# Query and key projections made once per token in the row passes and spread by copies, with three second-pass matmuls issued ahead of a step's first-pass ones

## The chip, the cores and the metric

One core of one Trainium2 chip runs the whole program in one launch. The metric is device time in microseconds (us), from the first to the last instruction of the launch, as the median of several runs. The engines are called PE (TensorE, matrix products), DVE (VectorE), ACT (ScalarE), POOL (GpSimd) and SP (SyncE, which here only issues copies). They run side by side, each through its own list of instructions in order, and meet at semaphores.

## The reference

Four sequences of 1024 tokens, 128 channels, float32. Two attention layers of 16 heads of 8 channels, the first causal with a linear position bias, the second full, and then a mixture of eight experts:

```python
x = L0_attn_x                                    # (4, 1024, 128)
x = x + layernorm(attn_causal_alibi(layernorm(x)))
u = layernorm(x)
u1 = u + layernorm(attn_full(u)) * ln1_g + ln1_b
u2 = u1 + layernorm(moe_top2_of_8(u1)) * ln2_g + ln2_b
x = x + layernorm(u2)
# both attentions, for 16 heads of 8 channels:
q, k, v = u @ Wq + bq, u @ Wk + bk, u @ Wv + bv
p = softmax(q k^T / sqrt(8) (+ slope * (i - j), causal))
out = (p v) @ Wo + bo
```

## The kernel before, in words

The program has five parts. A **first row pass** (`rows_pass`, tag `first`) reads the input, normalizes it, turns it so that channels lie on partitions, makes the values and leaves the turned input for all 4096 tokens in `turned` (a high and a low part, since a product is made as three matmuls of float32r parts: `three`). **Attention 1** (`attention`, tag `at1`, causal) follows, then a **second row pass** (tag `second`: output projection, norms, residual, turning, values), **attention 2** (tag `at2`, full) and the **tail** (experts), which the change does not touch.

A row pass goes over 8 groups of 512 tokens. The order of steps on each engine comes from the tables `ONLY_SPLIT` (first pass) or `JOIN` and `SPLIT_OFF` (second pass): step `s` of group `n` is sorted at time `n + table[s]`, so an engine's list interleaves steps of several groups.

An attention works in 16 **slots**: a slot is one sequence with four heads (`GH = 4`). Its 32 rows per head in `fq` (queries) and `km` (keys) hold the 8 query or key channels three times (high and low parts), two rows of position bias and two for the maximum. Each slot needs

- four **projections** (`proj`: key and query for both halves of the 1024 tokens). On PE three matmuls of 512 columns into a bank of the ring `a_bank` (a key of attention 1 has a fourth, for the bias), on ACT one pass into `u` (L443), on POOL three passes that split it into high and low rows (L596, L599, L606), and for keys four copies of 64 KB by SP (L627) that put each head's rows into `km`;
- the **first pass**, matmuls `a` (L367, 64 per slot in attention 2, 40 in attention 1, where diagonal blocks add two mask matmuls each, L372): scores with queries on partitions, of which DVE takes the row maximum (L498). They use a ring of four banks, so an `a` waits until DVE has read the fourth before it;
- the **second pass**, matmuls `b` (L395): scores again, with keys on partitions and the maximum subtracted, exponentiated by ACT (L454). They have three banks, so a `b` waits for the exponential of the third before it;
- `pv` (L412): the weighted values, four heads side by side in eight PE instructions;
- `mtr` and `otr`, small transposes for the maximum and for the output, with a division on DVE (`at_rec`, L526).

`Plan.body` writes a slot's order out: 12 steps in attention 1, 16 in attention 2. A step has the four `b` of one block of 128 keys, two to five `a` (spread over the steps by `weights`), at four of the steps a projection for the slot three ahead, and the `pv` of two blocks back. The `a` of the early steps (0 to 6 in attention 1, 0 to 10 in attention 2) belong to the next slot, those of the later ones to the slot after it:

```python
            out += bs[:1] + ass + bs[1:]
            ...
            for n, at in enumerate(self.proj_steps):
                if at == i and do_proj:
                    out.append(("proj", 3, n))
```

`Plan.prologue` makes the projections of the first three slots and the first slot's `a`. The first three batches' slots run in a loop over batches; the last four (slots 12 to 15) are written out. Slots 13, 14 and 15 have no projection, since there is no slot three ahead, and slot 15 has no `a` either.

## Time and profile before

| | |
|---|---|
| median of 3 runs | 2212.74 us (2209.97 to 2213.57) |
| the profiled execution | 2207.67 us, of which 2206.0 us are the span of the trace |
| PE busy | 1947.8 us (88% of the span) |
| DVE busy | 1661.0 us (75%) |
| ACT busy | 1342.6 us (61%) |
| POOL busy | 844.8 us (38%) |
| copies | 39656 packets, 41.98 MB |

A bracket behind a row of the timeline gives the idle time just before it and which instruction ended it. "x4" means that four instructions in a row were merged.

### The profile page before, as it was taken

To read this page: it belongs to the slowest core of one execution; us is meant where nothing else is said; L and a number is where in the kernel's file an instruction comes from. 1 tells how busy PE (TensorE), PEld (TensorE's weight loads), DVE (VectorE), ACT (ScalarE), POOL (GpSimd) and SP (SyncE) were. 2 spreads that over 40 slices of the span, in tenths; PEclk is the share of its full clock that TensorE was granted. 3 is DMA by queue.
4 is the path that set the end of the run, shared out by engine and by line. 5 is a ranking of instruction groups with operands and counts; after the bars stand their busy time and mean duration, and the time that the engine had idled before them with its cause. 6 is when DMAs were issued, how large, how long until landed. Compare 5 with 4: busy or idle time off the path is not lost. (4 is left out here: it accounts for less than half of the span.)

```text
span 2206.0 us, 41897 instructions
## 1 busy us (share of the span) xinstructions
PE 1947.8 (88%) x11036; PEld 1037.6 (47%) x11036; DVE 1661.0 (75%) x3185; ACT 1342.6 (61%) x2647; POOL 844.8 (38%) x816
## 2 busy tenths in 40 slices
PE   5899899899997699999999899999964999999996
PEld 4444444454443443333333334333323666666664
DVE  5677677677753778887888788888804999898986
ACT  4266666566765427766677676777763655555563
POOL 4455455545311342222222222220003466665554
PEclk7699999999986659999999999999996999999998
DMA  2100000000001200000000000000002100000000
GB/s 64 28 17 16 17 16 16 17 14 18 11 1 48 77 19 11 11 11 12 11 15 12 12 11 11 11 10 6 1 15 68 34 20 20 20 16 4 19 10 10
DMA packets 39656, 41.98 MB, mean 19 GB/s; under 512 B 6361, under 2 KB 24934, under 8 KB 39426
## 3 DMA queue, kind: packets, MB, share of 16 engines
q1 hardware_dynamic: 38544, 38.90, 6.4%
q8 instruction: 103, 1.69, 0.3%
q14 instruction: 127, 1.04, 0.2%
q10 hardware_dynamic: 882, 0.36, 0.1%
HBM read 14.07 MB, written 6.29 MB: 9 GB/s over the span
## 5 line engine op out<-in xcount | busy, mean ns | idle before, releaser
L498 DVE TENSOR_REDUCE at_mx<-at_a 128x1 f32<-128x512 f32 (+3 forms) x1664 | 997.6, 662 | 269.1 <-PE at_a L367 199.3
L454 ACT ACTIVATE at_probs<-at_b 128x512 f32<-128x512 f32 (+3 forms) x1792 | 868.2, 557 | 450.1 <-PE at_b L395 444.8
L395 PE MATMUL at_b<-at_fqm,km 64*128 64x512 f32 (+3 forms) x1792 | 632.3, 445 | 52.0 <-ACT at_probs L454 33.5
L395 PEld LDWEIGHTS at_b<-at_fqm,km 64*128 64x128 f32 x1792 | 295.9, 190 | 513.3 <-ACT at_probs L454 406.5
L367 PE MATMUL at_a<-km,at_fq 64*128 64x512 f32 (+2 forms) x1664 | 489.6, 458 | 37.6 <-DVE at_mx L498 29.3
L412 PE MATMUL at_pv<-at_probs,at_vst 128*32 128x512 f32 (+3 forms) x3584 | 449.8, 576 | 1.7 <-POOL at_probs L579 1.7
L596 POOL TENSOR_TENSOR at_hi<-at_u,split_sign 128x512 fp32r<-128x512 f32 x120 | 124.6, 1038 | 460.4 <-ACT at_u L443 406.9
L367 PEld LDWEIGHTS at_a<-km,at_fq 64*128 64x128 f32 x1664 | 238.9, 195 | 126.2 <-DVE at_mx L498 95.8
L1228 ACT ACTIVATE t_hid<-t_bank_h,b1t 128x512 f32<-128x512 f32 x256 | 173.9, 688 | 196.9 <-DVE t_hid_lo L1362 113.0
L1362 DVE TENSOR_TENSOR t_hid_lo<-t_hid,t_hid_hi 128x512 fp32r<-128x512 f32 x256 | 227.3, 923 | 13.9 <-ACT t_hid_hi L1235 11.8
L1396 POOL TENSOR_TENSOR t_hid_hi<-t_hid,pow_cols 128x512 fp32r<-128x512 f32 x112 | 140.8, 1272 | 130.4 <-ACT t_hid L1228 129.8
L579 POOL TENSOR_SCALAR_AFFINE_SELECT at_probs<-at_probs 128x512 f32<-128x512 f32 x128 | 81.1, 634 | 238.1 <-ACT at_probs L454 238.1
L443 ACT ACTIVATE at_u<-at_a,bias 128x512 f32<-128x512 f32 x128 | 88.7, 693 | 104.3 <-PE at_a L218 63.8
L216 PE MATMUL t_bank_y<-t_hid_hi,t_w2hi 128*128 128x512 f32 x256 | 107.0, 418 | 30.5 <-DVE t_weighed L1371 26.3
L599 POOL TENSOR_TENSOR at_part<-at_hi,split_sign 128x512 f32<-128x512 f32 x120 | 124.8, 1040 | 21.8 <-POOL at_hi L596 21.8
L412 PEld LDWEIGHTS at_pv<-at_probs,at_vst 128*32 128x32 f32 x3584 | 72.1, 109 | 112.0 <-ACT at_probs L454 53.7
L218 PE MATMUL t_bank_y<-t_hid_hi,t_w2lo 128*128 128x512 f32 x256 | 103.0, 402 | 0.0
L217 PE MATMUL t_bank_y<-t_hid_lo,t_w2hi 128*128 128x512 f32 x256 | 102.3, 400 | 0.0
L372 PE MATMUL at_a<-half_mask,half_ident 64*128 64x128 bf16 (+1 forms) x768 | 93.1, 249 | 2.9 <-issue 2.9
L526 DVE RECIPROCAL at_rec<-at_a 128x16 f32<-128x16 f32 x64 | 16.3, 254 | 94.0 <-PE at_a L419 92.6
L561 POOL COPY at_vst<-tokens 128x256 f32 (+1 forms) x32 | 12.9, 402 | 193.4 <-PE at_pv L412 192.9
L606 POOL TENSOR_TENSOR at_fk<-at_part,at_u 128x512 fp32r<-128x512 f32 x60 | 76.4, 1274 | 19.7 <-POOL at_part L599 19.7
(210 smaller groups left out, 2377.5 us busy)
## 6 DMA issues: line engine op xcount, KB each, us to landing
km<-at_fk SPq DMA_DIRECT2D x256, 64.0 KB, 2.0
t_raw<-L_ffn_W SPq DMA_DIRECT2D x16, 256.0 KB, 3.1
x_first<-L_attn_x SPq DMA_DIRECT2D x4, 512.0 KB, 7.6
second_x_in<-L_attn_x SPq DMA_DIRECT2D x8, 256.0 KB, 3.4
kept<-second_joined SPq DMA_DIRECT2D x8, 256.0 KB, 2.5
kept_u<-second_normed SPq DMA_DIRECT2D x8, 256.0 KB, 2.0
t_heads_in<-tokens SPq DMA_DIRECT2D x8, 256.0 KB, 2.7
t_u_in<-kept_u SPq DMA_DIRECT2D x8, 256.0 KB, 2.9
```

The source lines that it names most:

```text
L216: pe.matmul(out, a[0], b[0], start=start, stop=False)
L218: return pe.matmul(out, a[1], b[0], start=False, stop=stop)
L367: mm = pe.matmul(scores, fq[g][rows, qt * P:(qt + 1) * P], km[g][rows, first:first + k, kh * HALF:kh * HALF + w], start=True, stop=not dia ...
L395: mm = pe.matmul(out[:, 0:w], km[g][rows, j % 2, kt * P:(kt + 1) * P], fqm[g % 2][rows, q0:q0 + w], start=True, stop=True)
L412: mm = pe.matmul(pv_bank[HW * j:HW * (j + 1), HALF - w:HALF], vst[g % 2][:, kt, j, :], probs[n % PROBS][:, j, 0:w], start=(kt == 0), stop= ...
L454: act.activation(probs[t % PROBS][:, j, 0:w], b_bank[n % B_BANKS][:, 0:w], ACT.Exp).then_inc(exp_done, 1)
L498: dve.tensor_reduce(mx[:, kh, qt, heads[0]:heads[0] + k], scores[:, 0:k * w].rearrange("p (k w) -> p k w", k=k), AX.X, ALU.max).then_inc(a ...
L596: pool.tensor_tensor(hi[:, :], un[:, :], split_sign[:, 2:3].broadcast_to([P, HALF]), ALU.add).then_inc(pool_step, 1)
L599: pool.tensor_tensor(part[:, :], hi[:, :].bitcast(F32), split_sign[:, m:m + 1].broadcast_to([P, HALF]), ALU.mult).then_inc(pool_step, 1)
L1228: act.activation(hid[:, f, :], h_bank[f][:, :], ACT.Gelu, bias=b1t[:, f, e:e + 1]).then_inc(hidden["act"], 1)
L1362: dve.tensor_tensor(hid_lo[e % 2][:, f, :], hid[:, f, :], hid_hi[e % 2][:, f, :].bitcast(F32), ALU.subtract).then_inc(hidden["dve"], 1)
L1396: pool.tensor_tensor(out, a, b, op).then_inc(stage["pool"], 1)
```

## The change

1. The row passes make the projections of all 128 channels once: per group three matmuls for `q` and three for `k` (128 columns of weights instead of 32 rows per head in four slots), one ACT pass each (`q_out`, `k_out`), the high and low parts of the queries on DVE (`q_hi`, `q_lo`) and of the keys on POOL (`k_hi`, `k_lo`). They are kept in four arrays `packed`. To make room among the eight banks, the head transposes, the values and each projection have one bank instead of two, and `turned` is now a pair of buffers.
2. In the attentions a slot's `fq` and `km` rows are filled by 24 copies of 8 rows by 1024 columns (32 KB each), issued by SP at the start of a slot for the slot three ahead (`load`). All 24 must have landed before the slot's first `a`. Projections leave PE, ACT, DVE, POOL and the ring of banks. The loads of the first three slots stand in the prologue.
3. The position bias rows of `km` are computed once at the end of the first row pass (three DVE passes) and put in place by 16 copies of 4 rows; constant rows of `fq` are filled by POOL.
4. A step issues three `b`, its `a`, and then the fourth `b`.

```diff
@@ class Plan @@
-        weights = [4 + .6 * (i in self.proj_steps) - (i in self.o_steps) - 1.5 * (i in self.mt_steps) - .5 * (i == self.m_step)
+        weights = [4 - (i in self.o_steps) - 1.5 * (i in self.mt_steps) - .5 * (i == self.m_step)
                    for i in range(nq)]
...
+        out = [("load", 3, 0)] if do_load else []
...
-            out += bs[:1] + ass + bs[1:]
+            out += bs[:3] + ass + bs[3:]
...
-        out = [("proj", 0, n) for n in range(4)]
...
-        out += self.interleave(ahead[:early], [("a", 0, c) for c in range(self.na)])
+        out = [("load", s, 0) for s in range(3)]
+        out += [("a", 0, c) for c in range(self.na)]
@@ attention, tensor @@
-                            done(pe, split_done, 4, s, 2 * (qt // HQ) + 1)
-                            done(pe, keys_spread[kh], KEYS, s, KEYS - 1)
+                        if n == 0:
+                            done(pe, loaded, LOADS, s, LOADS - 1)
@@ attention, sync @@
+                    if ds == 3:
                         done(sp, b_made, NB, s - 4, NB - 1)
-                    done(sp, split_done, 4, s, n)
+                    done(sp, loaded, LOADS, s - 1, LOADS - 1)
+                    tokens = bass.ds(b * T, T)
                     for j in range(GH):
...
+                        for c in range(3):
+                            rows = slice(HW * j + c * DH, HW * j + (c + 1) * DH)
+                            sp.dma_start(fq[g][rows, :].bitcast(F32),
+                                         packed["q", QUERY_PARTS[c]][head, tokens].bitcast(F32)).then_inc(loaded, 16)
+                            sp.dma_start(km[g][rows, j % 2, :].bitcast(F32),
+                                         packed["k", KEY_PARTS[c]][head, tokens].bitcast(F32)).then_inc(loaded, 16)
@@ the tables of the row passes @@
 ONLY_SPLIT = {
+    "pe": {"turn": 1.6, "values": 2.85, "q": 4.05, "k": 4.1},
+    "act": {"root2": .5, "norm2": .9, "turned": 2.6, "high": 3.55, "q_out": 4.3, "k_out": 4.35},
+    "dve": {"stats2": 0, "scale2": .6, "values": 3.55, "low": 3.8, "q_hi": 4.7, "q_lo": 4.75},
+    "pool": {"k_hi": 4.7, "k_lo": 4.8},
 }
 SPLIT_OFF = {
+    "pe": {"turn": 3.22, "values": 3.5, "q": 4.1, "k": 4.15},
+    "act": {"root2": 2.47, "norm2": 2.85, "turned": 3.35, "q_out": 4.3, "k_out": 4.35},
+    "dve": {"stats2": 2.15, "scale2": 2.52, "values": 3.8, "low": 3.95, "q_hi": 4.6, "q_lo": 4.65},
+    "pool": {"high": 3.55, "k_hi": 4.6, "k_lo": 4.7},
 }
@@ rows_pass, tensor @@
+                else:
+                    if n == 0:
+                        extra.get("weights", lambda _: None)(pe)
+                    after(pe, "dve", "low", n)
+                    after(pe, "act", f"{step}_out", n - 1)
+                    m = "qk".index(step)
+                    mm = three(pe, qk_bank[step][0][:, :, :].rearrange("p a b -> p (a b)"),
+                               [part[:, m, :] for part in wqk], [part[i][:, :] for part in turned])
@@ build, the first pass's extras @@
+                sp.wait_ge(fixed_step, 3)
+                for h in range(H):
...
+                    sp.dma_start(km[g][rows, j % 2, :].bitcast(F32),
+                                 fixed[4 * h:4 * h + 4, :].bitcast(F32)).then_inc(fixed_put, 16)
+                sp.wait_ge(fixed_put, 16 * H)
...
+                for q in fq:
+                    pool.tensor_tensor(q[:, :], query_col[:, 0:1].broadcast_to([P, T]),
+                                       pow_cols[:, 3:4].broadcast_to([P, T]), ALU.add)
```

How it moves instructions on **PE in attention 2**, in the written-out slot 12 (`at_a`, `at_b`, `at_pv` are the banks; of before, two steps, the second with a projection):

```order
L395 MATMUL at_b<-at_fqm,km 128x512
L367 MATMUL at_a<-km,at_fq 128x512 x4
L395 MATMUL at_b<-at_fqm,km 128x512 x3
L412 MATMUL at_pv<-at_probs,at_vst 32x512 x4
L395 MATMUL at_b<-at_fqm,km 128x512
L367 MATMUL at_a<-km,at_fq 128x512 x5
L395 MATMUL at_b<-at_fqm,km 128x512 x3
L216 MATMUL at_a<-turned_hi,w_hi 128x512
L217 MATMUL at_a<-turned_lo,w_hi 128x512
L218 MATMUL at_a<-turned_hi,w_lo 128x512
L412 MATMUL at_pv<-at_probs,at_vst 32x512 x4
```

The same two steps of the changed kernel:

```order
L362 MATMUL at_b<-at_fqm,km 128x512 x3
L334 MATMUL at_a<-km,fq 128x512 x5
L362 MATMUL at_b<-at_fqm,km 128x512
L379 MATMUL at_pv<-at_probs,at_vst 32x512 x4
L362 MATMUL at_b<-at_fqm,km 128x512 x3
L334 MATMUL at_a<-km,fq 128x512 x4
L362 MATMUL at_b<-at_fqm,km 128x512
L379 MATMUL at_pv<-at_probs,at_vst 32x512 x4
```

The three projection matmuls are gone, the `a` stand between the third and the fourth `b`, and the steps with five `a` are others: 0, 2, 4 and 6 of a slot instead of 1, 3, 4, 6 and 9.

On **PE in the second row pass** the projections come between a group's values and the next group's turn (`bank_h`: heads turned, `bank_y`: output projection, `bank_n`: normalized rows turned, `bank_v`: values, `bank_q` and `bank_k`: projections). One group of before:

```order
L754 MATMUL second_bank_n<-ident,second_normed 128x128 x4
L748 MATMUL second_bank_y<-wo,second_heads_t 128x128 x4
L759 MATMUL second_bank_v<-wv,second_turned_1 128x128 x4
L743 MATMUL second_bank_h<-ident,tokens 128x128 x4
```

and of the changed kernel:

```order
L673 MATMUL second_bank_n<-ident,second_normed 128x128 x4
L667 MATMUL second_bank_y<-wo,second_heads_t 128x128 x4
L678 MATMUL second_bank_v<-wv,second_turned_1 128x128 x4
L662 MATMUL second_bank_h<-ident,tokens 128x128 x4
L208 MATMUL second_bank_q<-second_turned_hi,wqk_hi 128x512
L209 MATMUL second_bank_q<-second_turned_lo,wqk_hi 128x512
L210 MATMUL second_bank_q<-second_turned_hi,wqk_lo 128x512
L208 MATMUL second_bank_k<-second_turned_hi,wqk_hi 128x512
L209 MATMUL second_bank_k<-second_turned_lo,wqk_hi 128x512
L210 MATMUL second_bank_k<-second_turned_hi,wqk_lo 128x512
```

The six new matmuls need the low part of their own group's turned rows, and the next turn now stands behind them.

On **DVE in the second row pass** one group's round in the changed kernel, from one group's low part to the next one's, reads:

```order
L776 TENSOR_TENSOR second_turned_lo<-second_turned_0,second_turned_hi 128x512
L761 BN_STATS second_stats<-second_joined 128x6 x4
L765 BN_AGGR second_mean_var<-second_stats 128x2 x4
L769 RECIPROCAL second_scale<-second_root 128x4
L771 SCALAR_TENSOR_TENSOR second_shift<-second_mean_var,second_scale 128x4
L769 RECIPROCAL second_scale<-second_root 128x4
L771 SCALAR_TENSOR_TENSOR second_shift<-second_mean_var,second_scale 128x4
L780 CAST packed_q_hi<-second_q_out 128x512
L784 TENSOR_TENSOR packed_q_lo<-second_q_out,packed_q_hi 128x512
L748 TENSOR_TENSOR second_y<-second_bank_y,bo 128x512
L788 TENSOR_TENSOR tokens<-second_bank_v,bv 128x512
L761 BN_STATS second_stats<-second_y 128x6 x4
L765 BN_AGGR second_mean_var<-second_stats 128x2 x4
L776 TENSOR_TENSOR second_turned_lo<-second_turned_1,second_turned_hi 128x512
```

New in it are the two rows that write `packed`; the rest has the order of before.

## Rows read from the trace of the kernel before

**Rows 1.** Busy time by stage: stretch, its length, busy us (instructions) per engine, clock, copies.
```profile
0.00:48.50 48.50, 24.29 (x128) 21.62 (x128) 28.83 (x102) 24.89 (x59) 22.44 (x41) 0.84 0.28 73
...
107.70:690.00 582.30, 541.09 (x4000) 273.73 (x3996) 397.58 (x739) 370.46 (x840) 260.98 (x301) 0.95 0.06 14
690.00:750.00 60.00, 35.03 (x192) 29.52 (x192) 43.37 (x186) 39.20 (x97) 18.51 (x16) 0.74 0.33 106
...
824.00:1645.00 821.00, 756.04 (x4400) 312.10 (x4400) 634.24 (x1097) 578.57 (x1096) 179.97 (x170) 0.99 0.04 10
```

**Rows 2.** Timeline, DVE: the division at the end of slots 11 to 13, both attentions.
```profile
555.38 0.26 DVE L526 RECIPROCAL at_rec<-at_a 128x16 f32<-128x16 f32 x1
...
590.74 0.25 DVE L526 RECIPROCAL at_rec<-at_a 128x16 f32<-128x16 f32 x1
...
622.06 0.25 DVE L526 RECIPROCAL at_rec<-at_a 128x16 f32<-128x16 f32 x1
...
1460.13 0.26 DVE L526 RECIPROCAL at_rec<-at_a 128x16 f32<-128x16 f32 x1
...
1511.33 0.26 DVE L526 RECIPROCAL at_rec<-at_a 128x16 f32<-128x16 f32 x1
...
1558.69 0.26 DVE L526 RECIPROCAL at_rec<-at_a 128x16 f32<-128x16 f32 x1
```

**Rows 3.** Timeline of a step without first-pass matmuls, slot 15 of attention 2.
```profile
1612.16 0.73 PE L395 MATMUL at_b<-at_fqm,km 64*128 64x512 f32 x3
...
1613.35 0.50 PE L395 MATMUL at_b<-at_fqm,km 64*128 64x512 f32 x1 [0.46 <-ACT at_probs L454]
...
1614.77 0.73 PE L395 MATMUL at_b<-at_fqm,km 64*128 64x512 f32 x3
```

**Rows 4.** Timeline of a step with five first-pass matmuls, slot 13 of attention 2.
```profile
1512.97 10.68 DVE L498 TENSOR_REDUCE at_mx<-at_a 128x1 f32<-128x512 f32 x17 [1.06 <-PE at_a L367]
...
1514.82 0.49 PE L395 MATMUL at_b<-at_fqm,km 64*128 64x512 f32 x1
...
1516.33 0.49 PE L367 MATMUL at_a<-km,at_fq 64*128 64x512 f32 x1 [0.33 <-DVE at_mx L498]
...
1517.99 0.50 PE L395 MATMUL at_b<-at_fqm,km 64*128 64x512 f32 x1
```

**Rows 5.** Issues on SP in the timeline, and landing time on the page.
```profile
1224.08 2.41 SPq L627 DMA_DIRECT2D km<-at_fk  x4
...
1647.18 0.33 SPq L1669 DMA_DIRECT2D select<-const_select  x1
...
km<-at_fk SPq DMA_DIRECT2D x256, 64.0 KB, 2.0
```

**Rows 6.** Timeline, PE, prologues: first first-pass matmuls, and one projection.
```profile
58.60 0.39 PE L367 MATMUL at_a<-km,at_fq 64*128 64x256 f32 x2 [1.83 <-DMA km<-at_fk]
...
63.16 0.80 PE L216 MATMUL at_a<-turned_hi,w_hi 128*128 128x512 f32 x1
...
65.27 0.80 PE L367 MATMUL at_a<-km,at_fq 64*128 64x512 f32 x2
...
759.25 0.78 PE L367 MATMUL at_a<-km,at_fq 64*128 64x512 f32 x4 [2.91 <-DVE at_fk L488]
```

**Rows 7.** Groups of the second row pass by form: busy us, mean ns.
```profile
L827 DVE BATCH_NORM_STATS2 second_stats<-second_y 128x6 f32<-128x128 f32 x32 | 6.9, 278 | 0.1
...
L842 DVE TENSOR_TENSOR turned_lo<-second_turned,turned_hi 128x512 fp32r<-128x512 f32 x8 | 6.3, 785 | 0.0
```

**Rows 8.** Timeline, DVE: the last row step of the first row pass.
```profile
44.16 0.68 DVE L842 TENSOR_TENSOR turned_lo<-first_turned,turned_hi 128x512 fp32r<-128x512 f32 x1
```

**Rows 9.** The page's issues: size, and median us from issue to landing.
```profile
x_first<-L_attn_x SPq DMA_DIRECT2D x4, 512.0 KB, 7.6
```

**Rows 10.** Timeline of the first row pass, DVE beside POOL.
```profile
21.98 3.73 POOL L1599 TENSOR_TENSOR w_hi<-w,pow_cols 128x1024 fp32r<-128x1024 f32 x2
...
22.57 3.17 DVE L837 SCALAR_TENSOR_TENSOR first_shift<-first_mean_var,first_scale 128x4 f32<-128x4 f32 x1
```

More of the change, by code:

```diff
@@ L94, in __init__ @@
         o0 = self.half_end[0] + 1
-        free = [i for i in range(1, nq - 4) if i != o0]
-        self.proj_steps = [free[len(free) * i // 4] for i in range(4)]
         self.o_steps = (o0, nq - 1)
@@ L436, in emit @@
                     s = s0 + ds
[L437 to L446 removed]
+                    if what == "b":
                         t, j = n // GH, B_HEADS[n % GH]
@@ L564, in emit @@
             def emit(steps, s0, b0, g0, places, before):
-                if steps[0][1] == 0 and steps[0][0] == "proj":
+                if places is in_prologue:
                     stage_values(0, 0)
@@ L773, in _ @@
                     after(act, "pe", "project", n - 2)
-                    op = act.activation(heads_t[i][:, :], h_bank[i][:, :, :].rearrange("p a b -> p (a b)"),
+                    op = act.activation(heads_t[i][:, :], h_bank[0][:, :, :].rearrange("p a b -> p (a b)"),
                                         ACT.Identity)
+                elif step in ("q_out", "k_out"):
+                    k, m = step[0], "qk".index(step[0])
+                    if n == 0:
+                        extra.get("weights", lambda _: None)(act)
+                    after(act, "pe", k, n)
+                    after(act, "dve" if m == 0 else "pool", f"{k}_lo", n - 2)
+                    op = act.activation(out[k][i][:, :], qk_bank[k][0][:, :, :].rearrange("p a b -> p (a b)"),
+                                        ACT.Identity, scale=1.0 if m else SCALE, bias=bqk[:, m:m + 1])
                 elif step.startswith("root"):
```

350 lines of the change are left out of this document (116 added, 234 removed).

## The prediction

> **What bounds the kernel now.** I read the busy time by stage first. The two attentions take 582 and 821 us, the row passes only 48.5 and 60 [rows 1]. In the attentions PE is busy 93% and 92% of the time at a clock near full, DVE 68% and 77%, ACT 64% and 70% [rows 1]. No engine's throughput alone sets the pace, so I looked at single steps. Then I looked for a piece of the program in which the change is already half made, and there is one: slots 13 to 15 have no projection. The division that ends a slot marks slot lengths on DVE. Slot 12, with four projections, takes 590.74 − 555.38 = 35.36 us in attention 1; slot 13, with the same `a`, `b` and `pv` and no projection, takes 31.32. In attention 2 it is 51.20 and 47.36 [rows 2].
>
> What sets a step without projections? In slot 15 of attention 2 there are no `a` at all, and a step still takes 1614.77 − 1612.16 = 2.61 us [rows 3]. Its three free `b` go out at once, the fourth starts 1.19 later, released by ACT, and then `pv` holds PE until the next step. That is a chain of latencies (first `b`, its exponential, fourth `b`, `pv`), and a step with four `a` hides them inside it. A step with five `a` takes 1517.99 − 1514.82 = 3.17: its fifth `a` starts 1.51 in, when DVE has read the first, and three `b` stand behind it [rows 4]. DVE needs 10.68 / 17 = 0.628 us per `a` [rows 4].
>
> **The change, part by part.**
>
> *Projections leave the slots.* Slots 0 to 12 of both attentions lose what slot 13 lacks: 13 × 4.04 + 13 × 3.84 = 52.5 + 49.9 = **−102.4 us** [rows 2]. This contains PE's matmuls, ACT's pass, the bank and POOL's share. The new copies are absent in slot 13. They hang on SP, and are covered because they are issued when a slot begins for `a` that come more than a slot later. If that cover were gone, a slot would last as long as SP takes (a rival below).
>
> *Three `b` ahead.* The chain of 2.61 us starts with the first `b` and goes through the fourth, and both keep their places, so steps with four or fewer `a` gain nothing. Steps with five become four instead of five (one excess of 3.17 − 2.61 = 0.56 less), and in each of the four the last `a` has one `b` behind it instead of three, which I put at 0.1, since the `a` themselves start later by about the two `b` that were moved. DVE's 0.628 forbids more: 48 `a` in the first eleven steps are 30.1 us, those steps at 2.61 are 28.7. Together 1.0 per slot, 15 slots: −15. In attention 1, with narrower blocks and mask matmuls, I have no such clean pair of steps; I take a little less, 0.8 per slot, −12. Bounds: nothing at all, and double. **−27 us**.
>
> *Prologues.* An attention can start no `a` before 24 copies have been issued and landed. The price of an issue is not shown for copies of 8 rows from SBUF. Four copies of 32 rows inside SBUF take 2.41, 0.60 each; a copy of 8 rows of the same length from memory takes 0.33; landing takes 2.0 [rows 5]. I take the middle, 0.46, because one row shares the places and the other the shape: 24 × 0.46 + 2.0 = 13 us, with 10 and 16.4 as ends. Now the first `a` starts 10.1 and 9.3 us into the stage (58.60 and 759.25) [rows 1, 6], so it comes 3 and 4 us later. Against that a projection costs PE 65.27 − 63.16 = 2.1 us there with its bias matmul, about 1.6 without [rows 6]. In attention 1 seven of the first twelve lie on the path: −10 + 3 = −7. In attention 2 DVE's 64 × 0.628 = 40.2 us becomes the bound, so of eight projections (12.8 us) about half is recovered: −6.5 + 4. **−9.5 us**.
>
> *Second row pass.* Per group PE gets six matmuls of 0.53 at the low clock (2.11 / 4) [rows 6], half at the full one; the stage has 0.74 [rows 1], so 2.4 us. They need the group's low part, and the next turn is behind them. That closes a ring: low part, six matmuls 2.4, turn 0.7, ACT's copy 0.6 and root 0.3, DVE's scales 0.5, `q_hi` and `q_lo` 1.2, `y` and values 1.4, statistics (4 × 0.22 + 0.38) 1.25, low part 0.79. The last two are from their groups [rows 7], and I price the other 512-column passes at the same 0.6 to 0.8. That is 9.1 us per group. Now a group takes some 5.7: the stage has 60 us [rows 1], about 15 of them filling and draining. Four full groups × 3.4, three without `y` and statistics × 1.4, the first turn 4.4 later, the last group's projection, eviction and two splits 4.5 longer: 13.6 + 4.2 + 4.4 + 4.5 = **+27 us**. Ends: +10, if only PE's 1.6 at full clock per group counted, and +40.
>
> *First row pass.* The same ring is shorter: six matmuls 2.6, ACT's eviction and root 1.0, DVE's scale, two splits and low part 2.3: 6 us. Now a group takes 4.5: the last row step ends at 44.84 [rows 8], and the first can start when its input has landed, about 8.5 (0.8 of start and 7.6 to land [rows 9]), so (44.84 − 8.5) / 8. Eight groups × 1.5, and one unit of the table more until the last step: +12 + 6 = +18. Behind it the bias rows are put in place with nothing to hide them: 16 × 0.46 + 2 = 9.4. DVE's three closing passes replace three similar ones. **+27 us**.
>
> In these passes POOL matters too. A DVE instruction on 128 x 4 numbers took 3.17 us while POOL ran two large passes of 1024 columns in 3.73 together [rows 10], so DVE was held. POOL gets 2 passes per group more, and four of 1024 columns early in the first pass. The Trainium skill, "SBUF — State Buffer", on the shared port pair, says that a DVE instruction with two SBUF inputs and a POOL instruction exclude each other for a whole instruction. By that rule every new POOL pass may cost DVE its full length, and the trace agrees for this one instruction. I add nothing for it in the sum, since DVE waits for other engines a quarter of the second pass anyway; the full price is the fourth rival.
>
> Sum: −102.4 − 27 − 9.5 + 27 + 27 = −85 us. Against the profiled execution 2207.67 − 85 = 2123; the median of the runs lies 5.07 above that execution, so **2128 us**.
>
> **Rivals.**
>
> 1. *Favoured, 0.50:* as above, 2113 to 2143.
> 2. *Cheap row passes and copies, 0.17.* Copies issue at 0.33 (64 on the path × 0.13 = −8) and PE's clock rises with its work, so the ring gives back 1.2 per group, 16 × 1.2 = −19: 2101. For: the clock is 1.00 where PE is busiest. Against: it is 0.74 here with long waits, and they stay [rows 1].
> 3. *The order gives nothing or costs, 0.15.* The third `b` waits for the previous step's fourth exponential and now holds back the `a`, so DVE, with 0.628 per `a`, starves. In the step without `a` all three go out together, which speaks against it [rows 3]. The 27 us are lost: 2155.
> 4. *DVE held by POOL in the row passes, 0.10.* Two new POOL passes per group of 3.73 / 4 = 0.93 each fall on DVE fully, and the four large ones at 1.87: 16 × 1.87 + 4 × 1.87 = 37, so 2165. One row shows such a hold [rows 10]; against it, DVE is busy only 43.4 of 60 us in the second pass and could take it in its waits [rows 1].
> 5. *SP becomes the bound, 0.03, the other side.* Each slot needs 24 issues and the landing of all before the next 24. With p per copy a slot lasts 24p + 2. At 0.60 that is 16.4 us and hidden in 30.5; addresses are now computed from the loop's register. Only from p = 1.2 is attention 1 touched and from p = 1.45 the gain is gone; at 1.5 its slots take 38 instead of 30.5, 13 × 7.5 = +98: 2226. Nearest rows are 0.60 and 0.33 [rows 5].
> 6. *Others, 0.05*, in both directions, such as a different length of the loop's turnaround.
>
> The Trainium skill, "DMA: Bandwidth & Descriptors", in its measurements by size, calls transfers under 64 KB dominated by their descriptors, which speaks against 24 copies of 32 KB in place of 8 of 64. The rows have none of 32 KB inside SBUF. The 64 KB ones follow each other at 0.60 [rows 5]; if the price of a copy does not shrink with its bytes, the prologue term is the one at 0.60, 3.4 us more per attention.
>
> **How the numbers follow.** Likeliest is rival 1. Its own range is 2113 to 2143. For eight in ten the range takes in rivals 2 and 3 and the near side of 4: 2097 to 2164. What a measurement here can tell from no change is 0.2%, 4.4 us. Rivals 1 to 4 (0.92) end faster, and 0.03 of rival 6 does, so faster 0.95, within 0.2% 0.01, slower 0.04 (rival 5 and 0.01 of rival 6).
>
> **What would show it.** Slot lengths by the same division: 30.5 and 46.4 us in written-out slots (rival 3: 31.3 and 47.4; rival 5: above 32). Steps with four `a` still at 2.61, five near 3.08. First `a` about 13 us into each attention, with SP's issues near 0.46. Row passes of about 75 and 87 us; the spacing of turns in the second near 9 us, with PE waiting for the low part in front of the projections. The prediction fails if turns stay near 6 us apart, if DVE shows passes several times their length beside POOL, or if loads land after PE asks for them in the loop.

## The result and the profile after

The changed kernel takes **2155.11 us** (median of 4 runs, 2152.32 to 2157.07); the kernel before took 2211.35 beside it (4 runs, 2206.81 to 2213.57). The ratio is 0.9747, 95% interval 0.9727 to 0.9768: 2.5% faster. The predicted time was 2128 with a range of 2097 to 2164. The time lies in the range, but only two thirds of the 85 us came. The slots gave what I said in sum, 129.0 us for 129.4; what the change puts outside them cost 70.8 for 44.5. That the slots' sum fits is in part luck, as the last sections show.

Busy time by stage, kernel after; the columns are those of [rows 1]: stretch, its length, busy us (instructions) of PE, PE's weight loads, DVE, ACT and POOL, granted clock, DMA share, GB/s.
```profile
0.00:86.70 86.70, 39.29 (x144) 30.14 (x144) 45.66 (x117) 34.90 (x73) 40.04 (x34) 0.74 0.19 47
86.70:143.30 56.60, 35.62 (x156) 20.78 (x156) 31.50 (x60) 6.63 (x13) 5.69 (x11) 0.53 0.29 43
143.30:650.30 507.00, 492.74 (x3818) 245.14 (x3814) 375.78 (x740) 330.39 (x788) 84.55 (x139) 0.96 0.15 22
650.30:744.00 93.70, 54.30 (x240) 43.84 (x240) 56.51 (x200) 49.44 (x113) 44.04 (x36) 0.71 0.20 68
744.00:819.50 75.50, 54.09 (x110) 26.12 (x110) 50.06 (x86) 7.61 (x13) 3.83 (x8) 0.50 0.29 42
819.50:1586.80 767.30, 708.95 (x4244) 296.54 (x4244) 627.64 (x1098) 544.81 (x1044) 5.64 (x14) 0.99 0.09 14
```
Set against [rows 1], and against what each term said:

| stage | before | after | difference | said |
|---|---|---|---|---|
| first row pass | 48.5 | 86.7 | +38.2 | +27 |
| prologue 1 | 59.2 | 56.6 | −2.6 | −7 |
| slots, attention 1 | 582.3 | 507.0 | −75.3 | −64.5 |
| second row pass | 60.0 | 93.7 | +33.7 | +27 |
| prologue 2 | 74.0 | 75.5 | +1.5 | −2.5 |
| slots, attention 2 | 821.0 | 767.3 | −53.7 | −64.9 |
| tail | 561.0 | 563.8 | +2.8 | 0 |
| profiled span | 2206.0 | 2150.6 | −55.4 | −85 |

The lengths of before are those in [rows 1], the gaps between them, and the rest of the span. The first figure to look at is POOL in the slots of attention 2, down from 179.97 to 5.64 us: the projections' splits are gone. The cost is in the four short stages.

The divisions that end slots 11 to 13, in the timeline of DVE, after:
```profile
527.32 0.25 DVE L467 RECIPROCAL at_rec<-at_a 128x16 f32<-128x16 f32 x1
...
557.90 0.24 DVE L467 RECIPROCAL at_rec<-at_a 128x16 f32<-128x16 f32 x1
...
588.31 0.25 DVE L467 RECIPROCAL at_rec<-at_a 128x16 f32<-128x16 f32 x1
...
1407.02 0.25 DVE L467 RECIPROCAL at_rec<-at_a 128x16 f32<-128x16 f32 x1
...
1453.96 0.25 DVE L467 RECIPROCAL at_rec<-at_a 128x16 f32<-128x16 f32 x1
...
1500.81 0.25 DVE L467 RECIPROCAL at_rec<-at_a 128x16 f32<-128x16 f32 x1
```
Slot 13 now takes 588.31 − 557.90 = 30.41 us (31.32 in [rows 2]) and 46.85 (47.36). Slot 12, once 4.04 and 3.84 us longer than slot 13, is level with it: 30.58 and 46.94. The projections' part came as read from [rows 2]; what remains, 0.9 and 0.5 per slot, I had put down to the new order.

Second row pass, one group, timeline of all engines, after:
```profile
700.33 0.69 DVE L776 TENSOR_TENSOR second_turned_lo<-second_turned,second_turned_hi 128x512 fp32r<-128x512 f32 x1
...
701.07 0.79 PE L208 MATMUL second_bank_q<-second_turned_hi,wqk_hi 128*128 128x512 f32 x1 [4.48 <-DVE second_turned_lo L776]
...
703.80 0.78 PE L673 MATMUL second_bank_n<-ident,second_normed 128*128 128x128 f32 x4
704.04 0.69 ACT L707 ACTIVATE second_k_out<-second_bank_k,bqk 128x512 f32<-128x512 f32 x1 [0.59 <-PE second_bank_k L210]
...
705.11 0.29 ACT L712 ACTIVATE second_root<-second_mean_var,pow_cols 128x4 f32<-128x4 f32 x1
...
705.43 0.18 DVE L769 RECIPROCAL second_scale<-second_root 128x4 f32<-128x4 f32 x1 [2.96 <-ACT second_root L712]
705.64 0.71 DVE L771 SCALAR_TENSOR_TENSOR second_shift<-second_mean_var,second_scale 128x4 f32<-128x4 f32 x1
706.27 0.41 DVE L780 CAST packed_q_hi<-second_q_out 128x512 fp32r<-128x512 f32 x1
706.29 1.29 POOL L814 TENSOR_TENSOR packed_k_hi<-second_k_out,pow_cols 128x512 fp32r<-128x512 f32 x1
706.72 1.41 DVE L784 TENSOR_TENSOR packed_q_lo<-second_q_out,packed_q_hi 128x512 fp32r<-128x512 f32 x1
...
710.44 0.66 DVE L776 TENSOR_TENSOR second_turned_lo<-second_turned,second_turned_hi 128x512 fp32r<-128x512 f32 x1
```
This is the ring that I wrote down, and it takes 710.44 − 700.33 = 10.1 us instead of 9.1. Follow it: the low part, six matmuls (701.07 to 703.80), the turn, ACT, root, then DVE from 705.43 without a pause to the next low part. PE and DVE both wait on every round (4.48 and 2.96 us). The extra microsecond is DVE held beside POOL: `second_shift` takes 0.71 us here and 0.16 with POOL idle, `q_lo` 1.41 in place of 0.69.

SP and PE at the joint between the first row pass and attention 1, after:
```profile
74.53 10.09 SPq L1507 DMA_DIRECT2D km<-fixed  x16
86.72 0.67 SPq L540 DMA_DIRECT2D fq<-packed_q_hi  x1
87.45 0.65 SPq L542 DMA_DIRECT2D km<-packed_k_hi  x1
...
102.58 0.65 SPq L542 DMA_DIRECT2D km<-packed_k_hi  x1
...
104.99 0.59 PE L334 MATMUL at_a<-km,fq 64*128 64x256 f32 x2 [36.02 <-DMA km<-packed_k_hi]
...
762.33 1.22 PE L334 MATMUL at_a<-km,fq 64*128 64x512 f32 x4 [21.84 <-DMA km<-packed_k_hi]
```
The 24 copies follow each other at (102.58 − 87.45) / 22 = 0.69 us, not 0.46, and the first `a` starts 18.3 us into both attentions, where I said 13. PE sits idle for 36.02 us ahead of it in attention 1, since the bias rows come first and nothing runs beside them.

### The profile page after: what moved, and what is told of

It reads as the page before. It is cut to its first block and busy times, and to the rows that moved or that the text cites. A ratio compares the mean times of both kernels' runs of the same rounds, so it can differ in the third digit from the quotient of the medians.

```text
span 2150.6 us, 40102 instructions
## 1 busy us (share of the span) xinstructions
PE 1857.8 (86%) x10684; PEld 1001.0 (47%) x10684; DVE 1646.1 (77%) x3192; ACT 1272.8 (59%) x2549; POOL 488.6 (23%) x469
## 5 line engine op out<-in xcount | busy, mean ns | idle before, releaser
L411 ACT ACTIVATE at_probs<-at_b 128x512 f32<-128x512 f32 (+3 forms) x1792 | 858.2, 557 | 498.8 <-PE at_b L362 492.4
L362 PE MATMUL at_b<-at_fqm,km 64*128 64x512 f32 (+3 forms) x1792 | 541.2, 458 | 42.1 <-ACT at_probs L411 21.9
L334 PE MATMUL at_a<-km,fq 64*128 64x512 f32 (+2 forms) x1664 | 470.5, 447 | 82.6 <-DMA km<-packed_k_hi 57.9
L362 PEld LDWEIGHTS at_b<-at_fqm,km 64*128 64x128 f32 x1792 | 227.2, 189 | 485.4 <-ACT at_probs L411 404.1
L379 PE MATMUL at_pv<-at_probs,at_vst 128*32 128x512 f32 (+3 forms) x3584 | 445.2, 570 | 0.0
L334 PEld LDWEIGHTS at_a<-km,fq 64*128 64x128 f32 x1664 | 269.1, 195 | 183.7 <-DVE at_mx L439 94.9
L339 PE MATMUL at_a<-half_mask,half_ident 64*128 64x128 bf16 (+1 forms) x768 | 93.7, 250 | 0.0
L1188 ACT ACTIVATE t_hid_hi<-t_hid 128x512 fp32r<-128x512 f32 x144 | 81.4, 622 | 0.0
L208 PEld LDWEIGHTS t_bank_y<-t_hid_hi,t_w2hi 128*128 128x128 f32 x256 | 48.1, 188 | 58.4 <-DVE t_hid_lo L1315 30.8
L1331 DVE TENSOR_TENSOR t_acc<-t_acc,t_weighed 128x512 f32<-128x512 f32 x64 | 62.8, 982 | 2.4
L208 PE MATMUL t_bank_h<-t_w_t0hi,t_w1hi 128*128 128x512 f32 x128 | 56.5, 441 | 0.0
```

The costliest lines, as they stand in the source:

```text
L208: pe.matmul(out, a[0], b[0], start=start, stop=False)
L334: mm = pe.matmul(scores, fq[g][rows, qt * P:(qt + 1) * P], km[g][rows, first:first + k, kh * HALF:kh * HALF + w], start=True, stop=not dia ...
L339: mm = pe.matmul(scores[:, :, w - P:w], half_ident[rows, i, :], half_mask[rows, i, None, :].broadcast_to([PAIR, k, P]), start=False, stop= ...
L362: mm = pe.matmul(out[:, 0:w], km[g][rows, j % 2, kt * P:(kt + 1) * P], fqm[g % 2][rows, q0:q0 + w], start=True, stop=True)
L379: mm = pe.matmul(pv_bank[HW * j:HW * (j + 1), HALF - w:HALF], vst[g % 2][:, kt, j, :], probs[n % PROBS][:, j, 0:w], start=(kt == 0), stop= ...
L411: act.activation(probs[t % PROBS][:, j, 0:w], b_bank[n % B_BANKS][:, 0:w], ACT.Exp).then_inc(exp_done, 1)
```

## The experiments

My theory: (1) the slots' gain is real and nearly all the projections'; (2) the cost is one ring per row pass, closed by the places of q and k in the orders of the engines and stretched by POOL; (3) the rest is an issue price per copy, exposed where nothing runs beside. Rivals: the order carries much of the gain; DVE is simply held by POOL whatever the order; copies are bound by what moves them.

Every experiment starts from the changed kernel, but for one, which starts from the kernel before. "Ratio" is to the kernel before, run on the same chip. "Slot" is the time between two divisions inside the loop, "13" that of slot 13; "first `a`" is its start in attention 1, "gap" the time from the last division of attention 1 to the first `a` of attention 2.

| kernel | median us | ratio [95%] | first `a` | slot, 13 (att. 1) | gap | slot, 13 (att. 2) |
|---|---|---|---|---|---|---|
| changed | 2155.11 | 0.9747 [0.9727, 0.9768] | 105.0 | 31.17, 30.41 | 112.7 | 48.03, 46.85 |
| changed, again | 2155.89 | 0.9759 [0.9729, 0.9789] | 105.8 | 31.18, 30.39 | 112.5 | 48.03, 46.88 |
| order back | 2148.50 | 0.9715 [0.9693, 0.9738] | 104.6 | 31.41, 30.85 | 113.2 | 47.88, 46.79 |
| old spread of `a` | 2166.35 | 0.9794 [0.9768, 0.9820] | 105.5 | 31.31, 30.55 | 115.2 | 48.46, 47.31 |
| before, new order | 2217.77 | 1.0034 [1.0012, 1.0055] | 56.9 | 36.48, 30.87 | 69.6 | 52.33, 47.29 |
| two queues | 2140.88 | 0.9682 [0.9657, 0.9708] | 100.5 | 31.19, 30.43 | 108.9 | 48.04, 46.86 |
| turn ahead of q, k | 2149.66 | 0.9718 [0.9695, 0.9740] | 105.9 | 31.21, 30.41 | 106.9 | 48.05, 46.88 |
| POOL after `q_lo` | 2139.92 | 0.9682 [0.9660, 0.9703] | 97.1 | 31.18, 30.41 | 109.9 | 48.05, 46.83 |
| new tables | 2120.28 | 0.9581 [0.9556, 0.9607] | 89.9 | 31.20, 30.41 | 92.0 | 48.07, 46.90 |
| early copies | 2108.95 | 0.9535 [0.9512, 0.9558] | 74.3 | 31.20, 30.40 | 97.0 | 48.08, 46.83 |
| both | 2079.76 | 0.9409 [0.9384, 0.9434] | 64.8 | 31.20, 30.43 | 73.4 | 48.05, 46.87 |
| both, mixed order | 2076.21 | 0.9398 [0.9369, 0.9428] | 65.7 | 31.20, 30.41 | 74.0 | 47.89, 46.81 |

Three intervals carry a few microseconds of chance into each row: the loop's two turnarounds (33.9 to 36.5 us per slot in attention 1) and the last interval of attention 1 (25.4, 31.2 or 36.3). In the last one only the clock differs: over it the granted clock is 0.96 where it takes 25.4 us, 0.66 in the changed kernel (31.2), 0.51 with the new tables (36.3). The slot lengths repeat within 0.05.

**The order back.**
```diff
-            out += bs[:3] + ass + bs[3:]
+            out += bs[:1] + ass + bs[1:]
```

> The changed kernel with one second-pass matmul ahead of a step's first-pass ones, as before, in place of three; all else as changed. If the new order is worth what the slots of the changed kernel suggest (0.5 us a slot in attention 2, 0.9 in attention 1, over 15 slots each), the time rises by some 20 us to 2176, and attention 2's slots 12 to 13 read 47.4 in place of 46.9. If the order is worth nothing (all of the slots' gain is the projections'), 2155 within 4. If it is worth the 27 us of my sum, 2182. If three ahead in truth delays the first-pass matmuls and costs, under 2150.

Measured: 2148.50, ratio 0.9715. The theory that the order carries much of the gain falls, and so does my 20 us. Undoing it costs 0.24 us per slot in attention 1 and gives 0.15 back in attention 2; over 15 slots each that is +3.6 and −2.3, next to nothing. The time is at or below that of the changed kernel. Why, shows in the steps. Timeline of PE in attention 2 of the changed kernel, a step with four `a` and one with five:
```profile
1504.67 0.72 PE L362 MATMUL at_b<-at_fqm,km 64*128 64x512 f32 x3
1505.01 1.11 PE L334 MATMUL at_a<-km,fq 64*128 64x512 f32 x4
1505.85 0.50 PE L362 MATMUL at_b<-at_fqm,km 64*128 64x512 f32 x1
1506.28 1.07 PE L379 MATMUL at_pv<-at_probs,at_vst 128*32 128x512 f32 x8
1507.28 0.72 PE L362 MATMUL at_b<-at_fqm,km 64*128 64x512 f32 x3
...
1508.82 0.50 PE L334 MATMUL at_a<-km,fq 64*128 64x512 f32 x1 [0.30 <-DVE at_mx L439]
...
1510.47 0.72 PE L362 MATMUL at_b<-at_fqm,km 64*128 64x512 f32 x3
```
and a step with five `a` in the kernel with the order back:
```profile
1510.01 0.50 PE L362 MATMUL at_b<-at_fqm,km 64*128 64x512 f32 x1
...
1511.33 0.49 PE L334 MATMUL at_a<-km,fq 64*128 64x512 f32 x1 [0.30 <-DVE at_mx L439]
...
1513.21 0.50 PE L362 MATMUL at_b<-at_fqm,km 64*128 64x512 f32 x1
```
The four-`a` step lasts 2.61 us with PE issuing from end to end: 0.34 for three `b`, 0.84, 0.43 and 1.00. There is no pause in it that another order could fill. With five `a` the step lasts 1510.47 − 1507.28 = 3.19 in one order and 3.20 in the other: both wait the same 0.30 for DVE ahead of the fifth. The two `b` that no longer stand behind it now stand ahead of the first.

**The old spread of the first-pass matmuls.**
```diff
-        weights = [4 - (i in self.o_steps) - 1.5 * (i in self.mt_steps) - .5 * (i == self.m_step)
+        weights = [4 + .6 * (i in proj_steps) - (i in self.o_steps) - 1.5 * (i in self.mt_steps) - .5 * (i == self.m_step)
```

> The changed kernel with the first-pass matmuls spread over a slot's steps by the old weights (0.6 more in four steps), which the projections' places had set; nothing else. Slot 13 carries no projections before or after, yet fell from 31.32 to 30.85 and from 47.36 to 46.8 with the old order too. If the evener spread is that gain, it goes back by 0.5 us a slot, 15 us in all: 2170, slot 13 at 30.9 and 47.4. If the spread is worth nothing, 2155 within 4 and slot 13 as it is, 30.4 and 46.85.

Measured: 2166.35, ratio 0.9794 against 0.9747 and 0.9759. The even spread is worth 0.43 us per slot in attention 2 (48.46 against 48.03) and 0.13 in attention 1, some 8 us; I had expected 15. Taking the projections' weight from the planner moves `a` between steps, and this, not the place of the `b`, is what makes four steps with five `a` out of five in attention 2. My sum had that part, 0.56 per slot, but under the name of the order. It explains slot 13 in attention 2 (47.31 again, before 47.36). In attention 1 slot 13 owes 0.44 of its 0.91 to the order and 0.14 to the spread; the other 0.3 stays open.

**The new order alone, on the kernel before.** The same one line as above, the other way round, in the kernel before.

> The kernel before with the new order alone: three second-pass matmuls ahead of a step's first-pass ones, projections still in the slots. If the order does what undoing it in the changed kernel showed (attention 1 0.2 to 0.4 us a slot better, attention 2 0.15 worse), slot 13 reads 31.0 in attention 1 (31.32 before) and 47.5 in attention 2 (47.36), and the time is the old one within 5 us, ratio 1.000. If the order is worth more with projections about, as my sum had it (27 us), ratio 0.988. If it costs, because a projection now stands behind three matmuls, over 1.002.

Measured: ratio 1.0034, interval 1.0012 to 1.0055, a third of a per cent slower. Slot 13 came as expected (30.87 and 47.29). But slots with projections in attention 1 take 36.48 in place of 35.97, so with projections about, the order costs 0.5 us per slot, and without them it gains 0.24 in the loop and 0.45 in slot 13. I didn't follow this half microsecond to its wait; it stays open.

**Two queues for the prologue's copies.** The keys' 12 copies of a slot from SP, the queries' 12 from ACT, in the prologues only.
```diff
+                    elif what == "load" and places is in_prologue:
+                        done(act, loaded, LOADS, s - 1, LOADS - 1)
...
+                                act.dma_start(fq[ds][HW * j + c * DH:HW * j + (c + 1) * DH, :].bitcast(F32),
+                                              packed["q", QUERY_PARTS[c]][head, 0:T].bitcast(F32)).then_inc(loaded, 16)
```

> The three prologue loads of each attention pass are issued from two queues, the keys' 12 copies of a slot from SyncE and the queries' 12 from ScalarE, which is idle there; the slots' own loads and the bias rows are unchanged. If the 18.3 us ahead of the first first-pass matmul are 24 issues of 0.69 us on one queue, it starts after about 10 us and each prologue is 8 us shorter: 2139. If the copies are bound by what moves them (16 engines, or landing), the start stays at 18 and the time at 2155.

Measured: ratio 0.9682; the first `a` starts 13.0 us into attention 1 (87.5 to 100.5), and the two joints are 4.5 and 3.8 us shorter, half of what issue alone would give. The median, 2140.88, is close to the 2139 expected, but by luck: the joints account for 8.3 of its 14 us, and the rest is not located. SP's issues in this run:
```profile
92.50 1.00 SPq L548 DMA_DIRECT2D km<-packed_k_lo  x1
93.54 1.47 SPq L548 DMA_DIRECT2D km<-packed_k_hi  x2
```
An issue that took 0.65 alone takes 0.65 to 1.0 on SP beside the other queue and up to 1.46 on ACT, and the last copy's landing, 1.8 us behind its issue with one queue (102.58 + 0.65 to 104.99), is 2.2 behind it here. So the price per copy is neither SP's alone nor the movers' alone: two queues together issued 24 copies in 10.7 us, one per 0.45. What lengthens an issue beside the other queue is not shown.

**The turn ahead of q and k, second pass.**
```diff
-    "pe": {"turn": 3.22, "values": 3.5, "q": 4.1, "k": 4.15},
-    "act": {"root2": 2.47, "norm2": 2.85, "turned": 3.35, "q_out": 4.3, "k_out": 4.35},
+    "pe": {"turn": 3.22, "values": 3.5, "q": 4.3, "k": 4.35},
+    "act": {"root2": 2.47, "norm2": 2.85, "turned": 3.35, "q_out": 4.42, "k_out": 4.44},
```

> Second row pass only: TensorE takes a group's q and k matmuls behind the next group's turn instead of ahead of it (ScalarE's two evictions move behind the turned one accordingly). If the ring turn, turned, high, low, q and k, next turn sets the 10.1 us between groups, taking q and k (2.9 us) out of it gives 7.5 (VectorE's 7.1 busy is next) and the stage falls from 94 to some 75: 2137. If VectorE held by GpSimd is what sets the pace whatever TensorE's order, the spacing stays over 9.5 and the time within 4 of 2155.

Measured: ratio 0.9718. Only the first two groups came closer, and the gap shrinks by 5.8 us; from then on turns are 9.8 to 10.0 us apart (10.1 in the changed kernel), but for the last. My expectation of 7.5 fails. Timeline of this kernel:
```profile
701.59 0.69 DVE L776 TENSOR_TENSOR second_turned_lo<-second_turned,second_turned_hi 128x512 fp32r<-128x512 f32 x1
...
705.31 0.69 ACT L707 ACTIVATE second_k_out<-second_bank_k,bqk 128x512 f32<-128x512 f32 x1 [0.59 <-PE second_bank_k L210]
705.89 0.29 ACT L712 ACTIVATE second_root<-second_mean_var,pow_cols 128x4 f32<-128x4 f32 x1
...
711.47 0.66 DVE L776 TENSOR_TENSOR second_turned_lo<-second_turned,second_turned_hi 128x512 fp32r<-128x512 f32 x1
```
The turn is out of the ring, but a second one stands right behind it: ACT does `k_out` ahead of the root, and DVE waits for the root. Low part, six matmuls, `k_out`, root, DVE's run of passes, low part: 711.47 − 701.59 = 9.9 us. This alone can't tell a ring from a DVE that is simply held; the next two can.

**POOL after `q_lo`.**
```diff
                     after(pool, "act", "k_out", n)
+                    after(pool, "dve", "q_lo", n)
```

> Both row passes: GpSimd's k_hi and k_lo wait until VectorE has written q_lo of the same group. If VectorE's q_lo is held by GpSimd (1.4 to 2.3 us beside it, 0.69 alone) and lies on the ring, 0.7 us and more comes back in each of 16 groups: 2143. If the time only moves to GpSimd's later end (x1 and the next high wait for k_lo), 2155 or some us more.

Measured: ratio 0.9682, 15 us less than the changed kernel by the medians. The groups of `q_lo` by line in the changed kernel, both passes (instructions | busy us, mean ns):
```profile
L784 DVE TENSOR_TENSOR packed_q_lo<-first_q_out,packed_q_hi 128x512 fp32r<-128x512 f32 x8 | 10.0, 1246 | 0.3
...
L784 DVE TENSOR_TENSOR packed_q_lo<-second_q_out,packed_q_hi 128x512 fp32r<-128x512 f32 x8 | 9.9, 1232 | 0.3
```
and with the wait:
```profile
L784 DVE TENSOR_TENSOR packed_q_lo<-first_q_out,packed_q_hi 128x512 fp32r<-128x512 f32 x8 | 7.1, 889 | 0.3
...
L784 DVE TENSOR_TENSOR packed_q_lo<-second_q_out,packed_q_hi 128x512 fp32r<-128x512 f32 x8 | 5.5, 692 | 0.3
```
In the first pass two groups (turns at 38.02, 42.73 and 47.44) come 4.7 us apart instead of 7.5 and the first `a` 7.9 us earlier; in the second the gap shrinks by 2.8 only. There `second_shift` is still held (400 ns in the mean, with the wait and without), POOL's k passes end later, and its `x1` stands behind them. A wait *added* on POOL made the kernel faster, and the hold is real.

Not all of the first pass's 7.9 us is the hold, for the clock changed too. One group, from turn to turn, in the changed kernel, in the kernel with the order back (its first pass is that of the changed kernel, and so are its holds: `q_lo` 1.64 us, `first_shift` 0.70), and with the wait; the columns are those of [rows 1]:
```profile
46.97:54.42 7.45, 5.85 (x19) 4.47 (x18) 4.39 (x7) 4.19 (x9) 2.45 (x2) 0.50 0.01 2
...
47.30:53.50 6.20, 3.27 (x20) 2.52 (x19) 4.07 (x6) 4.01 (x9) 2.44 (x2) 1.00 0.00 0
...
42.73:47.44 4.71, 3.18 (x19) 2.52 (x18) 2.89 (x7) 4.11 (x10) 2.65 (x3) 1.00 0.00 0
```
The clock, 0.50 or 1.00, is worth 1.25 us of a group, the hold 1.49, which is just what `first_shift` (0.70 for 0.16) and `q_lo` (1.64 for 0.69) lose by it. Whether the shorter group brought the clock up is not shown: in the kernel with the order back it rose without any change to the pass.

**New tables for both row passes.** No instruction changed, only places. In the timeline of the second pass, k goes behind the next group's turn on PE, while q stays ahead of it (my expectation below names both); on DVE the low part goes ahead of `q_hi`; on ACT `k_out` goes from ahead of the root to behind it, between the two norms; on POOL `x1` goes ahead of `k_hi` and `k_lo`. In the first pass the next turn still stands behind q and k; ACT's root goes ahead of `k_out`, and DVE's low part ahead of `q_lo`. The two lines of the second pass that matter most:
```diff
-    "act": {"root2": 2.47, "norm2": 2.85, "turned": 3.35, "q_out": 4.3, "k_out": 4.35},
-    "dve": {"stats2": 2.15, "scale2": 2.52, "values": 3.8, "low": 3.95, "q_hi": 4.6, "q_lo": 4.65},
+    "act": {"root2": 2.62, "norm2": 2.95, "turned": 3.6, "q_out": 4.45, "k_out": 4.85},
+    "dve": {"stats2": 2.15, "scale2": 2.52, "values": 4.35, "low": 3.65, "q_hi": 4.65, "q_lo": 6.0},
```

> The changed kernel with only the tables of the two row passes rewritten, all instructions the same: q and k behind the next turn on TensorE, VectorE's low ahead of the group before's q_hi and q_lo, in the second pass ScalarE's q_out and k_out behind norm1, GpSimd's k_hi and k_lo later. If the spacing is a ring through all four engines that a place in their orders closes (low, q and k, k_out, root, norm, next turn), it opens: first-pass groups 5 us apart in place of 7.5, second-pass 6.7 in place of 10.1, and 35 to 45 us less: 2115. If it is VectorE held by GpSimd (the same pairs run whatever the order), the spacing stays within 1 us of 7.5 and 10.1, and the gain is under 12.

Measured: 2120.28, ratio 0.9581, 35 us less. Turns of the second pass in the timeline of this kernel:
```profile
669.82 0.65 PE L673 MATMUL second_bank_n<-ident,second_normed 128*128 128x128 f32 x4 [0.73 <-ACT second_normed L724]
677.61 0.66 PE L673 MATMUL second_bank_n<-ident,second_normed 128*128 128x128 f32 x4 [0.74 <-ACT second_normed L724]
```
and its group of `q_lo` in that pass:
```profile
L784 DVE TENSOR_TENSOR packed_q_lo<-second_q_out,packed_q_hi 128x512 fp32r<-128x512 f32 x8 | 10.4, 1305 | 0.0
```
Turns are 5.5 to 7.8 us apart in place of 10.1, and those of the first pass 4.2 to 4.7, in one case 5.8, in place of 7.5. And `q_lo` still takes 1305 ns beside POOL (1232 in the changed kernel). So the rival by which a held DVE sets the pace whatever the order falls: the holds stayed and the spacing went. In the second pass the clock has little part in it, 0.87 over the three groups that are 7.8 us apart against 0.84 in the changed kernel. In the first pass it is 1.00 throughout against 0.50, so of the way from 7.5 to 4.6 some 1.25 us are the clock's, and 1.6 the tables'.

The hold isn't free for that. In the groups 7.8 us apart DVE is busy 98% of the time, so now DVE itself sets the pace, with two held passes in each group:
```profile
678.38 1.70 DVE L784 TENSOR_TENSOR packed_q_lo<-second_q_out,packed_q_hi 128x512 fp32r<-128x512 f32 x1
...
683.55 1.51 DVE L780 CAST packed_q_hi<-second_q_out 128x512 fp32r<-128x512 f32 x1
```
Unheld they take 0.69 and 0.41: 2.1 us of a group. No run has both the new tables and POOL out of DVE's way.

**Early copies.** Slot 0's 24 copies are issued while the row pass runs (its tokens are groups 0 and 1), and the bias rows are computed behind `q_lo` of group 2.
```diff
+                after(sp, "dve", "q_lo", 1)
+                after(sp, "pool", "k_lo", 1)
+                load_slot0(sp, range(GH))
...
+                if (step, n) == ("q_lo", 2):
+                    extra.get("vector_end", lambda _: None)(dve)
```

> The changed kernel, but the 24 copies of slot 0 are issued while the row pass still runs (their tokens are groups 0 and 1), and in the first pass the bias rows are computed after group 2's q_lo and copied right behind them, instead of after the last group. If the 18.3 us ahead of each first first-pass matmul and the 16.6 us of bias rows at the end of the first pass (4.9 computed, 10.1 issued, 1.6 landed) are exposed work, some 12 of the 16.6 and nearly all of the 18.3 twice go: about 48 us less, 2107. If the copies slow the row passes by as much (SyncE also carries the second pass's rows, VectorE gets the 4.9 us in its ring), the gain is under 20: 2135 or more.

Measured: 2108.95, ratio 0.9535, 46 us less. The first `a` of attention 1 starts 30.7 us earlier, the gap to attention 2 is 15.7 shorter. So the copies and bias rows were exposed work; 3 us of it go into one longer group (10.6 in place of 7.5), where DVE makes the bias rows.

**Both.**

> The changed kernel with both: slot 0's copies and the bias rows early, and the rewritten tables of the two row passes. Apart they gave 36 us (tables) and 41 to 46 us (copies). If the two rings are apart the gains add: 2155 - 80 = 2075. If they share the end of the row passes (copies still on their way when the shorter pass is over: 24 of 0.69 us and 16 of 0.62 us are 26.5 us on SyncE, the first pass's packed rows are there from some 32 us), part is lost: 2085 to 2095.

Measured: 2079.76, ratio 0.9409, interval 0.9384 to 0.9434. The gains nearly add: 35 + 46 = 81, and 76 found. The first `a` starts at 64.8 us (58.60 in [rows 6]) and the gap is 73.4 (69.5 before). Of what the change had put outside the slots some 10 us are left, and this version beats both kernels, by 5.9% and 3.5%.

**Both, with attention 2 in the old order.**

> The same, with attention 2 back to one second-pass matmul ahead of a step's first-pass ones (attention 1 keeps three): with the order back, its slots took 47.85 in place of 48.02. If that holds, slots of attention 2 read 47.85 again and 2 us come back against the run beside it. If it was an accident of one kernel's instruction timing, no difference, or the other sign.

Measured: slots of attention 2 at 47.89 in place of 48.05, as expected; the ratio 0.9398 cannot be told from 0.9409. The trace also has the short last interval of attention 1 (25.4), in a part of the program that this edit does not touch.

**The changed kernel again.**

> The changed kernel itself once more, unedited, on the chip of the two others, so that their gain is measured against it on one chip. Ratio to the kernel before 0.9747 as at first, within 0.002. If the first measurement was off, the runs that undid a part of the change (0.9715 with the order back) need another reading.

Measured: 0.9759, interval 0.9729 to 0.9789; the slots repeat within 0.05 us, the first `a` of attention 1 within 0.8 and the gap within 0.2. The first measurement stands.

## Why the prediction was right, and where it was off

**Projections leave the slots: right.** Said −102.4, from slot 12 against slot 13. With order and spread taken out by the two experiments, projections are worth 35.97 − 31.17 − 0.24 − 0.13 = 4.4 us per slot in attention 1 and 52.23 − 48.03 − 0.43 + 0.15 = 3.9 in attention 2, where I had 4.04 and 3.84. Rival 5 did not occur: in the loop the issues are 0.79 us apart, and 24 of them (327.20 to 347.11 in the timeline of SP) and a landing hide in 31.

**Three `b` ahead: wrong.** The step that failed is "in each of the four the last `a` has one `b` behind it instead of three", with the 0.1 that it was to bring in each such step, and the 0.8 per slot taken over to attention 1. For the place of the `b` there is no such gain: undoing it changes the slots by +3.6 and −2.3 us, and the whole kernel is not slower. What is left of the −27 is its first part, five steps with five `a` become four: 0.56 per slot in the sum, 0.43 measured in attention 2 when the old spread is put back, and 0.13 in attention 1, some 8 us in all. The sum credited that to the order; it belongs to the planner's weights. So the term measured −10, not −27. I took 2.61 us for a chain of latencies, since a step without `a` lasts as long [rows 3]; in a step with four `a` it is PE's own stream, without a pause. The sign for it was there: steps with five `a` were to take 3.08 and take 3.19. Rival 3 had this outcome and its time, 2155, is the measured one, but not its mechanism: DVE does not starve, and the rest of its sum was off by errors that cancel.

That the slots came to 129 us all the same is luck. In attention 1 projections, order and spread make 13 × 4.4 + 3.6 + 2 = 63 of the 75 us; the other 12 lie in its stretches at the lower clock (the ends of its first slot, of the loop's rounds and of the last slot; rounds' ends 42.61 to 36.13, last interval 36.33 to 31.22), which partly repeat and partly are chance: the last interval alone gave 5, with the clock at 0.66 in place of 0.52. In attention 2 they make 13 × 3.9 + 6.5 − 2.3 = 55, and 53.7 came.

**Prologues: mis-sized.** Said −9.5, measured −1.1 (−2.6 and +1.5). The first `a` came 18.3 us in, not 13: the price of a copy was 0.69, above both rows between which I chose. A smaller slip works the other way: the seven projections on the path, at the sum's own 1.6 to 2.1 each, are 11 to 15 us and not 10. The sentence on what would follow, "if the price of a copy does not shrink with its bytes", was the right reading: 32 KB in 8 rows cost 0.69, 64 KB in 32 rows 0.60 [rows 5]. The Trainium skill, "DMA: Bandwidth & Descriptors", in its measurements by size, which are of copies from memory issued by GpSimd, calls transfers under 64 KB descriptor-dominated. The trace agrees in so far as half the bytes are no cheaper; that descriptors make the price is not shown, for a quarter of the rows is no cheaper either.

**Second row pass: right mechanism, mis-sized.** Said a ring of 9.1 and +27; measured 10.1 and +33.7. The held `second_shift` (0.55) and `q_lo` (0.7) are more than the difference; I had put the hold at nothing in the sum. The experiment with the turn first showed that I had named one ring where two of equal length lie.

**First row pass: mis-sized.** Said +18 until DVE's last row step, +9.4 for the bias rows. In the timeline, DVE's last split ends at 69.6 (44.84 in [rows 8]): +24.8. Its closing passes take 4.9 us in place of 3.7, two of them beside POOL. The copies take from 74.53 to the end of the stage, 12.2. The groups' ring is 7.45 us (turns at 46.97 and 54.42), not 6. Timeline of the first pass, after:
```profile
48.32 0.71 DVE L771 SCALAR_TENSOR_TENSOR first_shift<-first_mean_var,first_scale 128x4 f32<-128x4 f32 x1
...
49.09 1.41 POOL L819 TENSOR_TENSOR packed_k_lo<-first_k_out,packed_k_hi 128x512 fp32r<-128x512 f32 x1
...
49.40 1.64 DVE L784 TENSOR_TENSOR packed_q_lo<-first_q_out,packed_q_hi 128x512 fp32r<-128x512 f32 x1
```
The 1.45 us by which the ring is longer than said are these two: 0.71 for 0.16 and 1.64 for 0.69. Without the hold the ring is the 6 us said (7.45 − 1.49); the hold, which the sum put at nothing, is the step that failed for the groups, and the price of a copy for the bias rows (12.2 for 9.4). Rival 2 had the clock right in size, 1.2 us per group (1.25 in the rows above), but here the clock stayed at 0.50 in these groups. Rival 4 charged 37 us for the hold, and its sign came, a pass of DVE at four times its length (0.71 for 0.16). The added wait got 10.7 us back by the stages, a part of it the clock's, and 15 by the medians. The Trainium skill, "SBUF — State Buffer", on the shared port pair, has a DVE instruction with two SBUF inputs and a POOL instruction that reads SBUF exclude each other for the whole instruction. The trace agrees: in the rows above `q_lo` ends 0.54 us behind POOL's pass (50.50 and 51.04), and alone it takes 0.69, so most of it runs when POOL is done.

## What to carry to other kernels

Before an order is priced, look whether the engine that it reorders has a pause in the step at all; equal lengths of two steps do not mean equal causes. Work that leaves a long pipelined loop costs little by its busy time where it lands, and much by the ring that it closes there: write down which engine waits for which across one group, and place the new instructions so that the next group's first step does not stand behind them; then move the copies that follow up to where their data is first complete. Here that was worth more (76 us) than the change itself (56). And before a shorter group is credited to an edit, compare the granted clock of the two stretches.

## What the runs showed of the hardware that I had not expected

- The issue price of a copy inside SBUF does not follow its bytes: one starts 0.69 us after the other with 8 rows of 4 KB, 0.63 with 4 rows of 4 KB (10.09 / 16), 0.60 with 32 rows of 2 KB [rows 5], and a single issue took up to 1.46 with a second queue beside it (0.65 alone).
- POOL is held as well as DVE: `k_hi` takes 1.04 us alone and 1.29 beside DVE, and an instruction of DVE on 128 x 4 numbers took 0.71 in place of 0.16. With a wait added on POOL, so that the two take turns in one place, the median is 15 us lower.
- One interval, the last of attention 1, takes 25.4, 31.2 or 36.3 us in the traces of kernels whose instructions there are the same, at a granted clock of 0.96, 0.66 and 0.51. It alone moves a time by 5 to 11 us.
